# Turning the exponentials of an attention through scratch memory and VectorE instead of TensorE, with a second score tile in PSUM

## The chip, the core and the metric

One core of a Trainium2 chip runs the kernel alone, as one launch. The metric is the device time of that launch in microseconds (us). Engines are named as in the profile: PE (TensorE, with PEld for its weight loads), DVE (VectorE), ACT (ScalarE), POOL (GpSimd) and SP (SyncE, which here only waits for semaphores and issues DMAs). Each engine runs its own instruction list strictly in order; the lists meet only in semaphores.

## The reference, cut to what matters

The input is 16 images of 32x32 pixels and 128 channels, fp32. Each goes through two layers.

```
# layer 0: depthwise 3x3 convolution to 3C, 1x1 to 2C, gelu, 1x1 back to C, residual;
#          then 3x3 windowed local attention, residual
# layer 1: group norm (8 groups), then full attention over the 1024 pixels:
xf = xn.reshape(B, n, C)                                   # n = 1024
q, k, v = xf @ Wq + bq, xf @ Wk + bk, xf @ Wv + bv
attn = softmax(einsum('bnc,bmc->bnm', q, k) * C ** -0.5)   # 1024 x 1024 per image
out = einsum('bnm,bmc->bnc', attn, v) @ Wp + bp
return xn + out.reshape(B, H, W, C)
```

The change is in the full attention of layer 1: between the exponentials of a score tile, which come out with queries on the partitions, and the product with v, which needs keys on the partitions.

## The kernel before, in words

**Tiling.** The scores of one image are made in 8 tiles, `t` = 0 to 7, each 128 queries by 1024 keys (two PSUM banks). A tile goes through this chain: `scores(n, t)` on PE (6 matmuls); `row_max` on DVE (negated row maximum, out of PSUM); `exp` on ACT (PSUM to the SBUF tile `e`, with the row sums); `probs_t` on PE (8 transposes of 128x128 blocks of `e` into the PSUM tile `ps_t`); `et_hi_tile` on ACT (PSUM to `et_hi`, rounded to the fast matmul type fp32r); `et_lo_tile` on DVE (`ps_t` minus `et_hi`, the remainder). `values(n, j)` on PE multiplies the pair hi/lo of two tiles with the pair of v. Almost every product of the kernel is written as three fp32r matmuls over such hi/lo pairs (`mm3`, L438 to L443, which is why many groups of the profile stand at L441 to L443). On POOL one helper, `minus` (L1419, L1420), makes the remainders `t_lo`, `g_lo`, `h_lo` and `xn_lo`; both its operands lie in SBUF.

**Buffers.** Before the change there is one score tile in PSUM (`ps_s`), one tile `e`, one tile `ps_t`. `scores(t)` therefore waits for `exp(t-1)`, `exp(t)` for `probs_t(t-1)`, `probs_t(t)` for `et_lo_tile(t-1)`. `et_hi` and `et_lo` hold four tiles each, so tile `t` waits for `values` of tile pair `t/2 - 2`. Four more PSUM banks (`work`) are handed round by fixed plans (`BANK_PLAN`, `FILL_PLAN`, `DRAIN_PLAN`).

**Order.** The order of work of each engine is written out by hand as three lists of calls: `fill_program` (images 0 to 2 are started), `turn_program(it)`, run for it = 1 to 12, and `drain_program` (the last images). One turn works on four images at once: a = it (full attention, output), b = it + 1 (local attention, group norm, q, k, v of layer 1), c = it + 2 (convolution, gelu, q, k, v of layer 0), d = it + 3 (input and its Winograd transform). So in the steady state one turn finishes one image.

**Instructions of VectorE with both tensor operands in SBUF.** They matter below. In a turn there are ten larger ones: `transform_even` (2, L1602 and L1603), `transform_two` (2, L1612), `transform_ends` (2, L1621), `combine` (2, L1716), `combine_own` (2, L1723); and four tiny ones in the group norm (L1801, L1809, L1817, L1819). All others read PSUM with one operand, or have a single tensor operand.

**SP.** In a turn SP issues `store(a, 0)`, the four input loads of the next image (`load_x`), and `store(a, 1)`, each behind its wait.

```
            def probs_t(n, t):
                te.wait_ge(*e_ready.after(n, t))
                te.wait_ge(*et_lo_ready.after(n, t - 1))
                for kt in range(TILES):
                    mm = te.transpose(ps_t[:, kt * 128:(kt + 1) * 128], e[:, kt * 128:(kt + 1) * 128], ident)
```

Of the kernel before, what the change touches and what calls it, by code (L numbers as in the profile page):

```python
# [2227 lines left out]
```

## Time and profile before

| | us |
|---|---|
| three runs | 1071.11 median (1070.84 to 1073.47) |
| the profiled execution | 1070.88 |
| its span, first to last instruction | 1068.9 |
| PE busy | 1023.6 (96%) |
| DVE busy | 835.5 (78%) |
| ACT busy | 730.4 (68%) |
| POOL busy | 395.7 (37%) |
| mean granted clock of TensorE | 0.996 |

The page is read from the busy shares to the stages: the first score matmul of the drain stands at about 922 us, and a turn repeats every 63.7 us, so the twelve turns are by far the largest part. The chain that ended last is of little use here: much of it is "issue", time in which the engine waited for nothing that the profile shows.

### The profile page before, as it was taken

How to read it: one execution, taken by the hardware profiler on the slowest of the kernel's cores; microseconds unless marked ns; L12 is line 12 of the kernel's file. 1: busy time of each engine (PE TensorE's matmuls, PEld its weight loads, DVE VectorE, ACT ScalarE, POOL GpSimd, SP SyncE). 2: the span in 40 equal slices, each digit the busy share in tenths (PEclk: the TensorE clock that was granted, in tenths of full speed). 3: DMA queues.
4: the chain of work that ended last, by engine and by line, in shares of the span. 5: the costliest groups of instructions: out<-in, count | busy, mean ns of one | idle time of the engine just before them, and what ended most of it. 6: DMA issues, size and time to landing. Idle time of an engine off the chain costs nothing.

```text
span 1068.9 us, 21353 instructions
## 1 busy us (share of the span) xinstructions
PE 1023.6 (96%) x7092; PEld 937.6 (88%) x7092; DVE 835.5 (78%) x1628; ACT 730.4 (68%) x1382; POOL 395.7 (37%) x366
## 2 busy tenths in 40 slices
PE   4989999999999999999999999999999999999997
PEld 3877889899898999989899898989989899898986
DVE  6868888778787877887878788877877787777774
ACT  1576866757675776857767685776767667677754
POOL 4535250533507144260623516053260714423021
PEclk9899999999999999999999999999999999999999
DMA  5101010010201001020100101001010100000001
GB/s 91 21 2 21 2 30 11 10 31 1 40 0 29 10 10 29 0 39 0 24 16 10 29 0 29 10 10 29 0 39 0 29 10 10 10 1 11 11 11 30
DMA packets 85637, 18.64 MB, mean 17 GB/s; under 512 B 67552, under 2 KB 85472, under 8 KB 85600
## 3 DMA queue, kind: packets, MB, share of 16 engines
q1 hardware_dynamic: 84752, 17.77, 8.8%
q10 hardware_dynamic: 848, 0.39, 0.2%
q8 instruction: 22, 0.36, 0.1%
q14 instruction: 15, 0.12, 0.0%
HBM read 9.76 MB, written 8.39 MB: 17 GB/s over the span
## 4 chain that ended last, share of the span: by engine, by line
issue 43%; PE 29%; POOL 13%; DVE 9%; ACT 4%; DMA 0%; POOLq 0%; SPq 0%; DVEq 0%; ACTq 0%
PE work L441 6%; PE work L443 5%; PE work L442 5%; PE ps_t L604 4%; POOL t_lo L1420 3%; POOL d L1426 2%; ACT et_hi L1042 2%; POOL xn_lo L1420 2%; PE work L500 2%; DVE d L1602 2%; POOL g_lo L1420 2%; POOL r_tok L1474 1%; POOL r_tok L1477 1%; PE ps_s L441 1%; PE ps_s L443 1%
## 5 line engine op out<-in xcount | busy, mean ns | idle before, releaser
L1420 POOL TENSOR_TENSOR g_lo<-u,g_hi 128x512 fp32r<-128x512 f32 x60 | 76.8, 1283 | 415.1 <-ACT g_hi L951 415.0
L1854 DVE TENSOR_TENSOR et_lo<-ps_t,et_hi 128x1024 fp32r<-128x1024 f32 x128 | 156.1, 1220 | 52.1 <-ACT et_hi L1042 51.6
L1042 ACT ACTIVATE et_hi<-ps_t 128x1024 fp32r<-128x1024 f32 x128 | 130.9, 1022 | 91.0 <-PE ps_t L604 87.8
L441 PE MATMUL work<-t_lo,wc_hi 128*128 128x256 f32 x576 | 173.4, 301 | 4.4 <-DVE wc_lo L1668 4.4
L1848 DVE TENSOR_REDUCE nm<-ps_s 128x1 f32<-128x1024 f32 x124 | 150.9, 1217 | 22.8 <-PE ps_s L443 20.5
L443 PE MATMUL work<-t_hi,wc_hi 128*128 128x256 f32 x576 | 162.8, 283 | 0.0
L442 PE MATMUL work<-t_hi,wc_lo 128*128 128x256 f32 x576 | 162.6, 282 | 0.0
L441 PE MATMUL work<-et_lo,vv_hi 128*128 128x256 f32 x512 | 147.9, 289 | 0.2 <-ACT a_all L1049 0.2
L1032 ACT ACTIVATE e<-ps_s,nm 128x1024 f32<-128x1024 f32 x124 | 138.1, 1114 | 11.7 <-DVE nm L1848 9.2
L443 PE MATMUL work<-et_hi,vv_hi 128*128 128x256 f32 x512 | 144.4, 282 | 0.0
L442 PE MATMUL work<-et_hi,vv_lo 128*128 128x256 f32 x512 | 144.1, 281 | 0.0
L604 PE MATMUL ps_t<-const,e 128*128 128x128 f32 x1024 | 132.8, 273 | 3.4 <-DVE et_lo L1854 3.4
L604 PEld LDWEIGHTS ps_t<-const,e 128*128 128x128 f32 x1024 | 118.3, 141 | 17.3 <-ACT e L1032 3.6
L441 PEld LDWEIGHTS work<-t_lo,wc_hi 128*128 128x128 f32 x576 | 110.1, 191 | 5.5 <-issue 4.9
L442 PEld LDWEIGHTS work<-t_hi,wc_lo 128*128 128x128 f32 x576 | 110.1, 191 | 0.0
L443 PEld LDWEIGHTS work<-t_hi,wc_hi 128*128 128x128 f32 x576 | 109.6, 190 | 0.0
L441 PE MATMUL ps_s<-kk_lo,qq_hi 128*128 128x512 f32 x248 | 104.2, 420 | 0.4 <-ACT e L1032 0.3
L443 PE MATMUL ps_s<-kk_hi,qq_hi 128*128 128x512 f32 x248 | 98.2, 396 | 0.0
L442 PE MATMUL ps_s<-kk_hi,qq_lo 128*128 128x512 f32 x248 | 98.0, 395 | 0.0
L441 PEld LDWEIGHTS work<-et_lo,vv_hi 128*128 128x128 f32 x512 | 96.6, 189 | 1.3 <-issue 0.4
L442 PEld LDWEIGHTS work<-et_hi,vv_lo 128*128 128x128 f32 x512 | 96.5, 189 | 0.8
L443 PEld LDWEIGHTS work<-et_hi,vv_hi 128*128 128x128 f32 x512 | 96.4, 188 | 0.0
(184 smaller groups left out, 2415.7 us busy)
## 6 DMA issues: line engine op xcount, KB each, us to landing
x_in<-in_x SPq DMA_DIRECT2D x64, 128.0 KB, 3.4
out<-r_tok SPq DMA_DIRECT2D x32, 256.0 KB, 2.3
w_up_t<-in_L_conv_w_up SPq DMA_DIRECT2D x1, 384.0 KB, 3.8
const<-in_const ACTq DMA_DIRECT2D x1, 166.0 KB, 4.6
y<-in_L_conv_w_up ACTq DMA_DIRECT2D x1, 128.0 KB, 4.5
y<-in_L_conv_w_qkv SPq DMA_DIRECT2D x1, 128.0 KB, 4.7
const<-in_const ACTq DMA_DIRECT2D x1, 64.0 KB, 4.2
w_v<-in_L_conv_w_qkv SPq DMA_DIRECT2D x1, 64.0 KB, 2.8
```

The source lines that it names most:

```text
L441: te.matmul(dst, wh, xl, start=first, stop=False)
L442: te.matmul(dst, wl, xh, start=False, stop=False)
L443: return te.matmul(dst, wh, xh, start=False, stop=last)
L500: mm = te.matmul(bank("v", half, n)[:, t * 128:(t + 1) * 128], h[:, at:at + 128], w_v[:, :], start=True, stop=True)
L604: mm = te.transpose(ps_t[:, kt * 128:(kt + 1) * 128], e[:, kt * 128:(kt + 1) * 128], ident)
L1032: act.activation(e[:, :], score_tile(n, t)[:, :], ACT.Exp, bias=nm1[:, t:t + 1], accum_out=sum1[:, t:t + 1]) \
L1042: act.activation(et_hi[:, :, (t % 4) * 128:(t % 4 + 1) * 128], ps_t[:, :].rearrange("p (k c) -> p k c", k=TILES), ACT.Copy) \
L1420: return pool.tensor_tensor(dst, full, hi, ALU.subtract)
L1426: ins_ = pool.tensor_tensor(d2_of(n)[:, r], xp_of(n)[:, r + 2:r + 31:4, 1:1 + W], xp_of(n)[:, r:r + 29:4, 1:1 + W], ALU.subtract)
L1602: dve.scalar_tensor_tensor(d[:, 0], x[:, 1:30:4, 1:1 + W], -4.0, x[:, 3:32:4, 1:1 + W], ALU.mult, ALU.add)
L1848: dve.tensor_reduce(nm1[:, t:t + 1], score_tile(n, t)[:, :], AX.X, ALU.max, negate=True) \
L1854: dve.tensor_tensor(et_lo[:, :, cols_], ps_t[:, :].rearrange("p (k c) -> p k c", k=TILES), et_hi[:, :, cols_].bitcast(F32), ALU.subtract). ...
```

## The change

The eight PE transposes of a tile go. In their place the tile is written to a scratch tensor in DRAM and read back, so that one read brings 32 neighbouring keys' columns of all query blocks to one partition group, and a VectorE transpose (which works on blocks of 32x32) finishes the turn.

- `exp` writes `e` with its columns regrouped in runs of 32 (the same instruction, another output pattern). There are two tiles `e`, two tiles `e_by_keys`, two scratch areas `e_blocks`, used by t % 2.
- `move_out(n, t)` on SP waits for `exp(t)` and issues four stores of 32 partitions each (128 KB in runs of 1 KB). `move_in(n, t)` waits until all four have landed and issues one load of 512 KB (4 KB a partition).
- `et_turn(n, t)` on DVE waits for the load and transposes 128x1024 into the new SBUF tile `et_f`, in runs of 32.
- `et_hi_tile` on ACT now reads `et_f` in SBUF, not PSUM. `et_lo_tile` moves from DVE to POOL, reading `et_f` and `et_hi` in SBUF.
- The PSUM of `ps_t` becomes a second score tile: `scores(t)` waits for `exp(t-2)`. `exp(t)` waits for `et_turn(t-2)`.
- All lists and bank plans are written anew. `load_x(d)` stands in the turn where image d is transformed, no longer one turn ahead.

```diff
+        e = [sb(f"e_{k}", [128, PIX]) for k in range(2)]
+        e_by_keys = [sb(f"e_by_keys_{k}", [128, PIX]) for k in range(2)]
+        et_f = placed("et_f", [128, TILES, HALF], et_at + 4 * TILES * HALF)
...
-            return work_all[:, 0:PIX] if is_last(n) and t % 2 else ps_s
+            return (ps_s, ps_t)[t % 2]
...
+        e_blocks = nc.dram_tensor("e_blocks", (2, 128 * PIX), F32, kind="Internal").ap()
...
+            def move_out(n, t):
+                sp.wait_ge(*e_ready.after(n, t))
+                blocks = e_blocks[t % 2].rearrange("(a j q m) -> q j a m", a=4, j=32, q=4)
+                for part in range(4):
+                    sp.dma_start(blocks[part], e[t % 2][32 * part:32 * (part + 1), :].rearrange("j (a m) -> j a m", a=4)) \
+                      .then_inc(written[t % 2].handle, 16)
+
+            def move_in(n, t):
+                sp.wait_ge(*written[t % 2].after(n, t // 2))
+                sp.dma_start(e_by_keys[t % 2][:, :], e_blocks[t % 2].rearrange("(p c) -> p c", p=128)) \
+                  .then_inc(moved[t % 2].handle, 16)
...
-                if not is_last(n) or t == 0:
-                    te.wait_ge(*e_ready.after(n, t - 1))
...
+                te.wait_ge(*e_ready.after(n, t - 2))
...
-            def probs_t(n, t):
-                te.wait_ge(*e_ready.after(n, t))
-                te.wait_ge(*et_lo_ready.after(n, t - 1))
-                for kt in range(TILES):
-                    mm = te.transpose(ps_t[:, kt * 128:(kt + 1) * 128], e[:, kt * 128:(kt + 1) * 128], ident)
-                mm.then_inc(pe["t"].handle, 1)
...
             def exp(n, t):
                 act.wait_ge(*max1_ready.after(n, t))
-                act.wait_ge(*pe["t"].after(n, t - 1))
+                act.wait_ge(*et_ready.after(n, t - 2))
...
             def et_hi_tile(n, t):
+                cols_ = slice((t % 4) * 128, (t % 4 + 1) * 128)
+                act.wait_ge(*et_ready.after(n, t))
+                act.activation(et_hi[:, :, cols_], et_f[:, :, cols_], ACT.Copy).then_inc(et_hi_ready.handle, 1)
...
+            def et_lo_tile(n, t):
+                cols_ = slice((t % 4) * 128, (t % 4 + 1) * 128)
+                pool.wait_ge(*et_hi_ready.after(n, t))
+                minus(et_lo[:, :, cols_], et_f[:, :, cols_], et_hi[:, :, cols_].bitcast(F32)).then_inc(et_lo_ready.handle, 1)
...
+            def et_turn(n, t):
+
+                dve.wait_ge(*moved[t % 2].after(n, t // 2))
...
+                if t % 2 == 0:
+                    dve.wait_ge(*pe["pv"].after(n, t // 2 - 2))
                 cols_ = slice((t % 4) * 128, (t % 4 + 1) * 128)
...
+                dve.transpose(et_f[:, :, cols_].rearrange("p b (q j) -> p q b j", q=4),
+                              e_by_keys[t % 2][:, :].rearrange("p (q b j) -> p q b j", q=4, b=TILES)) \
+                   .then_inc(et_ready.handle, 1)
...
```

The new order of a turn, where the text below follows it (calls in their order, image letters as above, `out`/`in` for `move_out`/`move_in`):

```
SP:   out a0; in a0; out a1; in a1; out a2; out a3; in a2; in a3; load_x(d); out a4; out a5; in a4; in a5;
      out a6; out a7; in a6; in a7; store(a,0); store(a,1)
DVE:  row_max a1; local_mask_max b0; row_max a2; local_mask_max b1; local_rec b0; local_mask_max b2; halo_turn b0;
      local_rec b1; et_turn a0; row_max a3; sum_and_difference c(1); et_turn a1; halo_turn b1; sum_and_difference c(3);
      local_rec b2; row_max a4; local_mask_max b3; combine c(2); halo_turn b2; et_turn a2; row_max a5; et_turn a3;
      local_rec b3; combine c(1); combine_own c(0); combine_own c(3); end_row c(4); end_row c(5); halo_turn b3;
      y_half b0; row_max a6; et_turn a4; et_turn a5; row_max a7; y_half b1; h_half c0; channel_moments b;
      group_variance b; group_norm b; v_half c0; et_turn a6; output a0; et_turn a7; kk_lo b0; qq_lo b0; h_half c1;
      x_turn d0; kk_lo b1; x_turn d1; qq_lo b1; v_half c1; transform_even d; row_max b0; transform_two d; vv_lo b0;
      output a1; transform_ends d; vv_lo b1
ACT:  exp a1; ...; exp a2; local_scale b1; take c2; exp a3; local_scale b2; et_hi a0; et_hi a1; pt_pair b1;
      local_exp b3; exp a4; et_hi a2; pt_pair b2; exp a5; et_hi a3; local_scale b3; gelu c0; g_hi c0; gelu c1;
      a_part a0; g_hi c1; pt_pair b3; et_hi a4; exp a6; et_hi a5; exp a7; h_hi c0; gelu c2; ...; exp b0; ...
POOL: residual a0; et_lo a0; et_lo a1; et_lo a2; et_lo a3; g_lo c0; g_lo c1; et_lo a4; et_lo a5; inverse_deviation b;
      h_lo c0; g_lo c2; xn_lo b0; g_lo c3; xn_lo b1; et_lo a6; et_lo a7; h_lo c1; differences d; residual a1;
      transform d; t_lo d0; t_lo d1; t_lo d2
```

## Rows read from the trace of the kernel before

**Rows 1.** Stretches: us; PE, PEld, DVE, ACT, POOL busy; clock; DMA share; GB/s
```profile
404.30:468.20 63.90, 62.91 (x445) 58.05 (x444) 51.44 (x101) 45.06 (x86) 24.41 (x23) 1.00 0.08 16
851.30:1068.90 217.60, 206.71 (x1433) 187.72 (x1431) 158.78 (x310) 144.18 (x269) 61.79 (x55) 0.99 0.06 13
```

**Rows 2.** Timeline of SP's input loads (start, us, engine, line), five turns apart
```profile
276.62 2.55 SPq L381 DMA_DIRECT2D x_in<-in_x  x4
594.90 2.30 SPq L381 DMA_DIRECT2D x_in<-in_x  x4
```

**Rows 3.** Groups by line and form: busy us, mean ns, idle before and releaser
```profile
L1854 DVE TENSOR_TENSOR et_lo<-ps_t,et_hi 128x1024 fp32r<-128x1024 f32 x128 | 156.1, 1220 | 52.1 <-ACT et_hi L1042 51.6
L441 PE MATMUL ps_s<-kk_lo,qq_hi 128*128 128x512 f32 x248 | 104.2, 420 | 0.4 <-ACT e L1032 0.3
L1032 ACT ACTIVATE e<-ps_s,nm 128x1024 f32<-128x1024 f32 x124 | 138.1, 1114 | 11.7 <-DVE nm L1848 9.2 <-PE ps_t L604 2.2
L604 PE MATMUL ps_t<-const,e 128*128 128x128 f32 x1024 | 132.8, 273 | 3.4 <-DVE et_lo L1854 3.4
L1420 POOL TENSOR_TENSOR g_lo<-u,g_hi 128x512 fp32r<-128x512 f32 x60 | 76.8, 1283 | 415.1 <-ACT g_hi L951 415.0
L946 ACT ACT_TABLE_LOAD x18 | 23.1, 1283 | 0.3
L1596 DVE STREAM_TRANSPOSE xp<-x_in 128x512 f32<-128x512 f32 x30 | 21.0, 707 | 11.1 <-DMA x_in<-in_x 9.3
L1436 POOL TENSOR_TENSOR t_f<-d 128x256 f32<-128x256 f32 x15 | 11.4, 758 | 12.1 <-DVE d L1603 12.1
```

**Rows 4.** The output stores: KB each, median us to landing; issue durations in ns
```profile
out<-r_tok SPq DMA_DIRECT2D x32, 256.0 KB, 2.3
L397 SPq DMA_DIRECT2D out<-r_tok x32: 372/412/417, 139.6 to 1066.2; - x32
```

**Rows 5.** Half-microsecond stretches: under a weight load, under a store (columns as rows 1)
```profile
3.00:3.50 0.50, 0.00 (x0) 0.00 (x0) 0.00 (x0) 0.00 (x0) 0.09 (x2) 1.00 1.08 417
288.50:289.00 0.50, 0.50 (x4) 0.36 (x4) 0.16 (x1) 0.39 (x1) 0.50 (x1) 1.00 1.03 291
```

**Rows 6.** Timeline of POOL and DVE in one turn: start, us, engine, line
```profile
467.35 1.30 POOL L1420 TENSOR_TENSOR h_lo<-h,h_hi 128x512 fp32r<-128x512 f32 x1 [0.83 <-ACT h_hi L958]
467.43 1.49 DVE L1602 SCALAR_TENSOR_TENSOR d<-xp 128x256 f32<-128x256 f32 x1
468.85 0.41 DVE L1603 SCALAR_TENSOR_TENSOR d<-xp 128x256 f32<-128x256 f32 x1
...
473.23 2.53 DVE L1612 SCALAR_TENSOR_TENSOR t_f<-d 128x256 f32<-128x256 f32 x2
473.63 1.60 POOL L1420 TENSOR_TENSOR t_lo<-t_f,t_hi 128x512 fp32r<-128x512 f32 x1
...
477.94 1.18 DVE L1621 SCALAR_TENSOR_TENSOR t_f<-d 128x256 f32<-128x256 f32 x2
...
512.25 1.30 POOL L1474 TENSOR_TENSOR r_tok<-vv_hi,vv_lo 128x512 f32<-128x512 f32 x1
512.26 0.69 DVE L1790 TENSOR_TENSOR y<-work,h 128x512 f32<-128x512 f32 x1 [0.41 <-PE work L545]
513.62 1.28 POOL L1477 TENSOR_TENSOR r_tok<-r_tok,bp_row 128x512 f32<-128x512 f32 x1
513.96 0.96 DVE L1801 SCALAR_TENSOR_TENSOR moments<-moments 128x1 f32<-128x1 f32 x1
```

**Rows 7.** Durations of two lines, ns min/median/max, over all images
```profile
L1716 DVE SCALAR_TENSOR_TENSOR u<-u x30: 670/680/840, 39.3 to 941.8; 128x512 f32<-128x512 f32 x30
L1801 DVE SCALAR_TENSOR_TENSOR moments<-moments x16: 219/955/1019, 81.2 to 1014.3; 128x1 f32<-128x1 f32 x16
```

**Rows 8.** Timeline of ACT: first and last exponential after the twelve turns
```profile
929.46 1.10 ACT L1032 ACTIVATE e<-ps_s,nm 128x1024 f32<-128x1024 f32 x1
1054.98 1.11 ACT L1032 ACTIVATE e<-work,nm 128x1024 f32<-128x1024 f32 x1
```

More of the change, by code:

```diff
@@ L406, in fill_program @@
                 load_x(2)
+                move_out(0, 0)
+                move_in(0, 0)
+                move_out(0, 1)
+                move_in(0, 1)
+                move_out(0, 2)
+                move_in(0, 2)
+                move_out(0, 3)
+                move_in(0, 3)
+                move_out(0, 4)
+                move_in(0, 4)
+                move_out(0, 5)
+                move_out(0, 6)
+                move_in(0, 5)
+                move_in(0, 6)
                 load_x(3)
+                move_out(0, 7)
@@ L408, in fill_program @@
+                move_in(0, 7)
                 store(0, 0)
-                load_x(4)
                 store(0, 1)
             def turn_program(it):
-                a, d = it, it + 3
+                a, b, c, d = it, it + 1, it + 2, it + 3
+                move_out(a, 0)
+                move_in(a, 0)
+                move_out(a, 1)
+                move_in(a, 1)
+                move_out(a, 2)
+                move_out(a, 3)
+                move_in(a, 2)
+                move_in(a, 3)
+                load_x(d)
@@ L414, in turn_program @@
+                move_out(a, 4)
+                move_out(a, 5)
+                move_in(a, 4)
+                move_in(a, 5)
+                move_out(a, 6)
+                move_out(a, 7)
+                move_in(a, 6)
+                move_in(a, 7)
                 store(a, 0)
-                if has_next(d + 1):
-                    load_x(d + 1)
                 store(a, 1)
             def drain_program():
-                store(B - 3, 0)
-                store(B - 3, 1)
-                store(B - 2, 0)
@@ L423, in drain_program @@
-                store(B - 2, 1)
+                move_out(B - 3, 0)
+                move_in(B - 3, 0)
+                move_out(B - 3, 1)
+                move_in(B - 3, 1)
+                move_out(B - 3, 2)
+                move_in(B - 3, 2)
+                move_out(B - 3, 3)
+                move_in(B - 3, 3)
+                move_out(B - 3, 4)
+                move_in(B - 3, 4)
+                move_out(B - 3, 5)
+                move_in(B - 3, 5)
+                move_out(B - 3, 6)
+                move_in(B - 3, 6)
@@ new lines, in drain_program @@
+                move_out(B - 3, 7)
+                store(B - 3, 0)
+                move_in(B - 3, 7)
+                move_out(B - 2, 0)
+                move_in(B - 2, 0)
+                move_out(B - 2, 1)
+                move_in(B - 2, 1)
+                move_out(B - 2, 2)
+                move_in(B - 2, 2)
+                move_out(B - 2, 3)
+                move_in(B - 2, 3)
+                move_out(B - 2, 4)
+                store(B - 3, 1)
+                move_in(B - 2, 4)
+                move_out(B - 2, 5)
@@ new lines, in drain_program @@
+                move_in(B - 2, 5)
+                move_out(B - 2, 6)
+                move_in(B - 2, 6)
+                move_out(B - 2, 7)
+                move_in(B - 2, 7)
+                move_out(B - 1, 0)
+                store(B - 2, 0)
+                move_out(B - 1, 1)
+                move_in(B - 1, 0)
+                move_in(B - 1, 1)
+                move_out(B - 1, 2)
+                move_out(B - 1, 3)
+                move_in(B - 1, 2)
+                move_in(B - 1, 3)
+                store(B - 2, 1)
@@ L424, in drain_program @@
+                move_out(B - 1, 4)
+                move_out(B - 1, 5)
+                move_in(B - 1, 4)
+                move_in(B - 1, 5)
+                move_out(B - 1, 6)
+                move_out(B - 1, 7)
+                move_in(B - 1, 6)
+                move_in(B - 1, 7)
                 store(B - 1, 0)
                 store(B - 1, 1)
-            fill_program()
-            turn_program(1)
-            with sp.Fori(2, B - 4) as it:
-                turn_program(it)
-            turn_program(B - 4)
@@ L432, in _ @@
-            drain_program()
+            run(sp, fill_program, turn_program, drain_program)
             sp.wait_ge(*stored.after(B - 1, 1))
@@ new lines, in fill_program @@
+                local_exp(1, 1)
+                local_scale(1, 0)
+                take(2, 0, 1)
+                exp(0, 1)
+                t_hi_part(2, 1)
+                q_half(1, 1)
+                local_scale(1, 1)
+                pt_pair(1, 0)
+                exp(0, 2)
+                pt_pair(1, 1)
+                local_exp(1, 2)
+                et_hi_tile(0, 0)
+                t_hi_part(2, 2)
+                local_scale(1, 2)
+                take(2, 2, 3)
+                local_exp(1, 3)
@@ L1189, in fill_program @@
+                et_hi_tile(0, 1)
+                exp(0, 3)
+                et_hi_tile(0, 2)
+                vv_hi_half(0, 1)
+                exp(0, 4)
                 pt_pair(1, 2)
+                local_scale(1, 3)
                 gelu(2, 0)
+                pt_pair(1, 3)
+                g_hi_part(2, 0)
                 gelu(2, 1)
-                g_hi_part(2, 0)
-                et_hi_tile(0, 2)
+                gelu(2, 2)
                 g_hi_part(2, 1)
-                local_exp(1, 3)
@@ L1236, in turn_program @@
                 a, b, c, d = it, it + 1, it + 2, it + 3
+                exp(a, 1)
+                local_exp(b, 0)
+                local_scale(b, 0)
+                local_exp(b, 1)
+                local_exp(b, 2)
+                pt_pair(b, 0)
+                take(c, 0, 1)
+                exp(a, 2)
+                local_scale(b, 1)
+                take(c, 2, 3)
+                exp(a, 3)
+                local_scale(b, 2)
                 et_hi_tile(a, 0)
-                exp(a, 1)
-                take(c, 0, 1)
@@ new lines, in drain_program @@
+                exp(B - 3, 5)
+                g_hi_part(B - 1, 2)
+                exp(B - 3, 6)
+                h_hi_half(B - 1, 0)
+                et_hi_tile(B - 3, 4)
+                a_part(B - 3, 0)
+                xn_hi_half(B - 2, 0)
+                xn_hi_half(B - 2, 1)
+                a_part(B - 3, 1)
+                g_hi_part(B - 1, 3)
+                q_half(B - 1, 0)
+                k_half(B - 1, 0)
+                qq_hi_half(B - 2, 0)
+                kk_hi_half(B - 2, 0)
+                kk_hi_half(B - 2, 1)
@@ L2148, in drain_program @@
-                halo_turn(B - 1, 3)
-                et_lo_tile(B - 2, 5)
-                y_half(B - 1, 0)
+                local_rec(B - 1, 0)
+                et_turn(B - 2, 0)
+                local_rec(B - 1, 1)
+                halo_turn(B - 1, 0)
+                local_mask_max(B - 1, 2)
+                row_max(B - 2, 3)
+                halo_turn(B - 1, 1)
+                local_rec(B - 1, 2)
+                et_turn(B - 2, 1)
+                halo_turn(B - 1, 2)
+                local_mask_max(B - 1, 3)
@@ L2151, in drain_program @@
+                vv_lo_half(B - 2, 0)
+                row_max(B - 2, 4)
+                et_turn(B - 2, 2)
+                local_rec(B - 1, 3)
+                output(B - 3, 1)
+                row_max(B - 2, 5)
+                halo_turn(B - 1, 3)
+                y_half(B - 1, 0)
+                vv_lo_half(B - 2, 1)
+                et_turn(B - 2, 3)
                 y_half(B - 1, 1)
                 channel_moments(B - 1)
+                row_max(B - 2, 6)
                 group_variance(B - 1)
+                et_turn(B - 2, 4)
@@ L2181, in drain_program @@
+                et_turn(B - 1, 6)
+                et_turn(B - 1, 7)
                 output(B - 1, 0)
[L2182 removed]
                 output(B - 1, 1)
```

1032 lines of the change are left out of this document (478 added, 554 removed), and 59 rows, old and new, of tables (BANK_PLAN, DRAIN_PLAN, FILL_PLAN).

## The prediction

> **What bounds the kernel now.** I read the busy shares of the page first: PE 96%, DVE 78%, ACT 68%, POOL 37%. An average over stages proves nothing, so the next view is the busy time by stretch. Input loads five turns apart give the turn: (594.90 - 276.62) / 5 = 63.66 us [rows 2]. In one such turn PE is busy 62.9 of 63.9 us, DVE 51.4, ACT 45.1, POOL 24.4 [rows 1]. So in the steady state PE sets the pace and the others wait for it. Twelve turns are 764 of the 1070.9 us. The sum below is made against the profiled execution, 1070.88 us (span 1068.9), which lies 0.23 us under the median of the runs. The other 305 us are the fill and the last images; there too PE is busy, for 206.7 of the last 217.6 us [rows 1].
>
> **What goes.** The 1024 transposes keep PE busy for 132.8 us [rows 3], 1.04 us a tile, 8.3 us a turn. PE's floor of a turn falls from 62.9 to 54.6 us. If PE alone mattered the turns would give back 12 x 9 = 108 us.
>
> **What comes, by engine, per turn.**
>
> *DVE.* `et_lo` goes (1.22 us a tile), `et_turn` comes. The trace has a transpose of 128x512 at 0.707 us [rows 3], also with output in runs of 32. Bounds for 128x1024: 1.22 us if the second 512 columns cost what they cost an ordinary instruction (0.69 us for 512 [rows 6], 1.22 for 1024: +0.53 [rows 3]), twice 0.707 = 1.41 at the other end. I take 1.24, next to the row of the same width: a change of +0.2 us a turn, at most +1.5.
>
> *ACT.* `et_hi` reads SBUF in place of PSUM: nothing that matters in 45 us. But gelu and exp now alternate twice a turn (gelu, exp a6 and a7, gelu, exp b0) and a table load takes 1.28 us [rows 3]: two more, +2.6 us. ACT stands at 48 us, hidden, except that one load falls ahead of `exp a6`.
>
> *POOL.* Eight `et_lo` of 128x1024. The trace has 0.758 us for 256 and 1.283 for 512 elements [rows 3]: 1.283 + 2 x 0.525 = 2.33 us (2.57 if it were twice the 512). That is 18.7 us; POOL goes from 24.4 to 43 us a turn. It still has slack, yet this is the costly edit, for the next reason.
>
> *The lock between POOL and DVE.* A DVE instruction with both operands in SBUF stands still while POOL works. L1602 took 1.49 us from 467.43, until `h_lo` on POOL had ended at 468.65; its twin L1603 behind it took 0.41 [rows 6]. Two L1612 across POOL's instructions took 2.53 us, the pair L1621 with POOL idle 1.18 [rows 6]. L1801, 0.22 us when free, has a median of 0.955 [rows 7]. The addition out of PSUM at 512.26 took its usual 0.69 beside POOL [rows 6]. The Trainium skill's page SBUF — State Buffer, section Who interferes with whom, has this as a rule: a VectorE instruction with two SBUF inputs and a GpSimd instruction that reads SBUF lock each other out for the whole instruction. By that rule `et_lo` on DVE (one operand in PSUM) never took part, and `et_lo` on POOL does, for 2.33 us at a time; the trace agrees with the first half (the row at 512.26), and no run here shows the second yet.
>
> Priced from the rows: fourteen such instructions a turn. Today they lose (1.49 - 0.41) + (2.53 - 1.18) + (0.96 - 0.22) = 3.2 us. If they met POOL at random, each would lose the sum of half the squares of POOL's durations over the turn: (15 instructions of 512 elements, 6 of 256) (15 x 1.28² + 6 x 0.76²) / 2 = 14.0; 14.0 / 63.7 x 14 = 3.1 us, just about what they lose. After the change 8 x 2.33² / 2 = 21.7 is added: 35.7 / 62 x 14 = 8.1 us. But they don't meet at random: in the new order `et_hi` a2 and a3 follow closely on `et_turn` a2 and a3, and `combine` and two `combine_own` come right behind on DVE, so two of these wait for nearly a whole `et_lo` (4.3 us); `channel_moments` follows `et_lo` a5. Placed by hand so, the losses come to 13. I take 10, between the two, against 3.2 now.
>
> *The round trip through DRAM.* An issue takes SP 0.41 us [rows 4], some 0.48 with what lies between; four are 1.9. A store of 256 KB lands 2.3 us after its issue [rows 4], of which some 0.9 is data at 291 GB/s [rows 5]; so 1.4 fixed, and the last 128 KB of four lands 1.4 + 0.4 after its issue: 3.2 us for `move_out`. `move_in`: 512 KB at 417 GB/s, the best stretch of the trace [rows 5], is 1.26 us, at 291 it is 1.8: 2.7 to 3.2 after issue, I take 3.0. Together 6.3 us. Bounds: 5.7 if `move_out` takes 3.0 and the load runs at 417 GB/s; 8.7 if the last store takes the 2.3 us of one twice its size (3.7 in all) and the load, next to other traffic, half of 291 GB/s (5.0).
>
> Where does it show? `exp(t)` waits for `et_turn(t-2)`, so two tiles are under way, and SP holds `in a2` behind `out a3`, `in a4` behind `out a5`, `in a6` behind `out a7`. After `et_turn a1` ends, `exp a3` takes 1.3, `out a3` 1.9 of issue, `in a2` 3.0: `et_turn a2` can start 6.2 us later, and DVE has some 4.7 us of work till then (the calls between them in its new list, at the durations of the same calls in the turn of rows 6, as are the next two figures; `combine` with 0.68 [rows 7] is the typical one): a wait of 1.5. From `et_turn a3` to a4: 6.4 us against 6.4 of work: none. From a5 to a6: `et_hi`, a table load and two exponentials stretch it to 9.4, against 7: 2.5, which the locks of the group norm fill. At the turn's seam `out a0` queues on SP behind `store(a-1, 1)`, which waits for `output`; DVE has 8 us of work before it asks: none. What is queued behind a waiting `et_turn` is all of DVE: `row_max`, hence `exp`; the convolution's sums, hence gelu. I keep 3.5 us of waits and gaps a turn beside the locks. `load_x(d)`, moved into this turn, costs SP 2.5 us ahead of `out a4`, which isn't ready before, and its reader comes half a turn later: nothing, or half a us if its packets delay `out a4`.
>
> *Second score tile.* PE waits 0.4 us in all before its first score matmul [rows 3]: worth nothing today; it covers the longer chain of tomorrow.
>
> **Sum.** DVE of a turn: 51.4 - 3.2 (locks now) + 0.2 + 10 (locks after) + 3.5 = 61.9 us, above PE's 54.6: DVE with its waits becomes what ends last. Twelve turns: 12 x (61.9 - 63.7) = -21. After the last turn there is little to hide the round trip behind: the exponentials of 23 tiles lie 125.5 us apart there, first to last [rows 8]. A pair's loop is now 1.25 (exp) + 3.8 (two `move_out` issued) + 0.5 (load issued) + 3.0 + 1.24 = 9.8 us; 11.5 pairs make 113, 12 less. The tail behind the last `exp` gets the round trip and a slower `et_lo` for PE's transposes, +6. About -5. The fill, PE busy too, gives perhaps -5. Total 1070.9 - 31 = 1040 us.
>
> **Rivals.**
> *A, forecast:* the locks eat most of what PE gives back. Turn 60 to 64, 1015 to 1064 us.
> *B, the locks stay small,* as today's 3.2 us or little more, because DVE stands in waits anyway when POOL works. For it: the losses of the group norm are partly covered. Against: `combine` stands right behind `et_turn`. DVE 55 to 58, PE's floor 54.6: turn 57, 12 x -6.7 - 10 = -90: 980 us.
> *C, slower: the round trip is the bound.* Place: `et_turn` a2, a4, a6 on DVE, and the pairs of the last images. Each us beyond 6.3 adds about 3 us a turn, since three of the four pairs have no slack, 36 in all, and 12 us at the end: 1040 + 48x. It decides from 6.95 us; 7.5 gives 1098, 8 gives 1122. For it: five DMAs a tile where a turn had six in all, and stores, loads and input on one queue. Against: the traffic asked is 8 MB a turn, 135 GB/s, and 291 and 417 were seen.
> *D, the transpose takes 1.41,* not 1.24: +1.4 us a turn moves A by 16 us, still faster; that the PE work goes is sure from the diff.
>
> **Chances.** A 0.45, B 0.27, C 0.22 (locks of 13 with a round trip of 6.6 end there too), the rest around no change. What a measurement of this kernel can tell from no change is about 0.3%, 3.2 us. Faster 0.70 (B, most of A, D), same 0.08, slower 0.22. Likeliest 1040, its own range 1010 to 1064; with B down to its middle and C up to 7.5 us of round trip, 975 to 1100.
>
> **What would show it.** Right: PE busy near 890 us with waits in every turn; L1854 gone and a DVE transpose of 1.2 to 1.3 us x128; POOL `et_lo` at 2.3 us; `combine`, `combine_own` and L1801's successors with medians 1 us and more above 0.68 and 0.22 [rows 7]; turn 60 to 64 us. Wrong: `combine` at 0.68 (B); `et_turn` waiting for the DMA several us a turn (C); loads landing after 4 us or more (C); ACT or SP busy without a gap, which no step above allows for.

## The result, and the profile after

1129.45 us (median of 4 runs, 1122.80 to 1130.03) against 1071.14 for the kernel before on the same chip: the ratio is 1.0525, 95% interval 1.0483 to 1.0567. The change made the kernel slower by 58 us; 1040 was forecast, and the range ended at 1100.

First the busy shares of the page of the kernel after (1129.47 us, span 1127.7):

```profile
PE 965.2 (86%) x6068; PEld 852.9 (76%) x6068; DVE 905.2 (80%) x1628; ACT 749.6 (66%) x1402; POOL 714.5 (63%) x494
```

PE lost the transposes and is no longer what ends last; no engine is above 86%. So no engine's busy time explains the loss by itself, and the waits have to be looked at. To place them, the span is cut at `channel_moments` of image 2 and of image 12, ten turns apart (the `memset` of `stat_mark` on DVE marks them). First the kernel before, then after: us from and to, length, busy PE, PEld, DVE, ACT, POOL, granted clock, DMA share, GB/s.

```profile
195.48:832.05 636.57, 626.96 (x4402) 577.94 (x4402) 511.94 (x1002) 448.03 (x851) 241.84 (x221) 1.00 0.09 17
```

```profile
207.50:874.86 667.36, 585.82 (x3761) 519.44 (x3760) 561.14 (x1002) 468.87 (x871) 445.38 (x300) 0.98 0.53 142
```

Three stretches make up the 58.8 us between the two spans: up to image 2, +12.0 (207.50 - 195.48); the ten turns, +30.8 (66.74 us a turn instead of 63.66); the rest, +16.0 (252.8 instead of 236.9). In a turn DVE is now busy for 56.1 us (51.2 before) and idle for 10.6. The waits of DVE in those ten turns (engine, tile and line, who ended the wait: us in total, times, longest):

```profile
DVE et_f L1934 <- DMA e_by_keys<-e_blocks: 56.3, 39, 3.0
DVE r_tok L1947 <- POOL r_tok L1511: 17.9, 10, 1.9
DVE max_mark L1838 <- ACT pn L1023: 10.6, 10, 1.1
DVE gn L1891 <- POOL gn L1487: 6.6, 10, 0.7
DVE g_mom L1881 <- PE work L640: 6.0, 10, 0.8
...
```

`et_turn` (L1934) waits 5.6 us a turn for its load, and 4.1 us more are spread over four other places. The largest of these, `r_tok`, is new: `output` waits there for POOL's `residual`, which stands behind the last `et_lo` in POOL's list (17.9 us in ten turns; before the change DVE stood idle for 0.7 at this place). The groups that answer to [rows 3] and [rows 7] (busy us, mean ns, idle before):

```profile
L1449 POOL TENSOR_TENSOR et_lo<-et_f,et_hi 128x1024 fp32r<-128x1024 f32 x128 | 313.9, 2464 | 251.3 <-ACT et_hi L1073 251.3
L1934 DVE STREAM_TRANSPOSE et_f<-e_by_keys 128x1024 f32<-128x1024 f32 x128 | 157.5, 1237 | 103.6 <-DMA e_by_keys<-e_blocks 103.3
...
L1797 DVE SCALAR_TENSOR_TENSOR u<-u 128x512 f32<-128x512 f32 x30 | 56.4, 1919 | 0.0
...
L1790 DVE SCALAR_TENSOR_TENSOR u<-u 128x512 f32<-128x512 f32 x30 | 32.5, 1088 | 0.0
```

The transpose takes the 1.24 us that was forecast, `et_lo` 2.46 where 2.33 was. `combine_own` (L1797) needs 1.92 us, 0.68 when nothing holds it [rows 7]: the lock is there. The transfers (KB each, median us from issue to landing) took longer than forecast:

```profile
e_blocks<-e SPq DMA_DIRECT2D x512, 128.0 KB, 2.6
e_by_keys<-e_blocks SPq DMA_DIRECT2D x128, 512.0 KB, 4.1
```

One turn shows the trip tile by tile. SP's queue, then DVE (start, us):

```profile
417.87 15.00 SPq L399 DMA_DIRECT2D out<-r_tok  x2
433.26 1.80 SPq L410 DMA_DIRECT2D e_blocks<-e  x4
437.10 0.34 SPq L415 DMA_DIRECT2D e_by_keys<-e_blocks  x1
437.56 1.88 SPq L410 DMA_DIRECT2D e_blocks<-e  x4
442.44 0.34 SPq L415 DMA_DIRECT2D e_by_keys<-e_blocks  x1
443.70 6.45 SPq L410 DMA_DIRECT2D e_blocks<-e  x8
450.26 0.39 SPq L415 DMA_DIRECT2D e_by_keys<-e_blocks  x1
```

```profile
441.19 1.25 DVE L1934 STREAM_TRANSPOSE et_f<-e_by_keys 128x1024 f32<-128x1024 f32 x1 [1.18 <-DMA e_by_keys<-e_blocks]
...
445.82 1.25 DVE L1934 STREAM_TRANSPOSE et_f<-e_by_keys 128x1024 f32<-128x1024 f32 x1 [1.08 <-DMA e_by_keys<-e_blocks]
...
454.61 1.25 DVE L1934 STREAM_TRANSPOSE et_f<-e_by_keys 128x1024 f32<-128x1024 f32 x1 [2.81 <-DMA e_by_keys<-e_blocks]
```

Tile a1: stores issued from 437.56, load at 442.44, transpose at 445.82, 8.3 us behind the first store. Tile a2: the first four of the eight stores at 443.70, its load only at 450.26, because SP first waits for the exponential of a3 and issues that tile's stores; the transpose begins 10.9 us behind the first store and DVE has stood for 2.81 us.

### The profile page after: what moved, and what is told of

The parts are those of the page before. It is cut to its first block, busy times and chain, and to the rows that moved or that the text cites. A ratio compares the mean times of both kernels' runs of the same rounds, so it can differ in the third digit from the quotient of the medians.

```text
span 1127.7 us, 20253 instructions
## 1 busy us (share of the span) xinstructions
PE 965.2 (86%) x6068; PEld 852.9 (76%) x6068; DVE 905.2 (80%) x1628; ACT 749.6 (66%) x1402; POOL 714.5 (63%) x494
## 4 chain that ended last, share of the span: by engine, by line
POOL 36%; issue 33%; DMA 6%; DVE 3%; PE 3%; SPq 1%; ACT 1%; POOLq 1%; DVEq 0%; ACTq 0%
POOL et_lo L1449 16%; POOL g_lo L1449 4%; POOL d L1455 4%; DMA e_by_keys<-e_blocks 3%; POOL r_tok L1508 3%; DMA e_blocks<-e 2%; POOL h_lo L1449 2%; POOL xn_lo L1449 2%; POOL t_lo L1449 2%; POOL r_tok L1511 2%; SPq L410 1%; DVE et_f L1934 1%; PE work L528 1%; PE work L530 1%; PE work L529 1%
## 5 line engine op out<-in xcount | busy, mean ns | idle before, releaser
L1449 POOL TENSOR_TENSOR et_lo<-et_f,et_hi 128x1024 fp32r<-128x1024 f32 x128 | 313.9, 2464 | 251.3 <-ACT et_hi L1073 251.3
L1934 DVE STREAM_TRANSPOSE et_f<-e_by_keys 128x1024 f32<-128x1024 f32 x128 | 157.5, 1237 | 103.6 <-DMA e_by_keys<-e_blocks 103.3
L528 PE MATMUL work<-t_lo,wc_hi 128*128 128x256 f32 x576 | 168.8, 293 | 10.3 <-DVE nm L1841 7.4
L1073 ACT ACTIVATE et_hi<-et_f 128x1024 fp32r<-128x1024 f32 x128 | 133.6, 1055 | 29.4 <-DVE et_f L1934 29.4
L1066 ACT ACTIVATE e<-ps_s,nm 128x1024 f32<-128x1024 f32 x64 | 71.4, 1115 | 80.2 <-DVE et_f L1934 76.7
L1066 ACT ACTIVATE e<-ps_t,nm 128x1024 f32<-128x1024 f32 x64 | 71.2, 1113 | 50.8 <-DVE et_f L1934 40.2
L528 PE MATMUL ps_s<-kk_lo,qq_hi 128*128 128x512 f32 x128 | 57.6, 450 | 31.9 <-ACT e L1066 31.6
L1922 DVE TENSOR_REDUCE nm<-ps_s 128x1 f32<-128x1024 f32 x64 | 77.4, 1210 | 3.8 <-PE ps_s L530 3.6
L1449 POOL TENSOR_TENSOR t_lo<-t_f,t_hi 128x512 fp32r<-128x512 f32 x48 | 61.1, 1297 | 26.6 <-ACT t_hi L959 26.6
L1922 DVE TENSOR_REDUCE nm<-ps_t 128x1 f32<-128x1024 f32 x64 | 76.5, 1195 | 0.0
```

The source lines that it names most:

```text
L528: te.matmul(dst, wh, xl, start=first, stop=False)
L1066: act.activation(e[t % 2][:, :].rearrange("p (a b i) -> p b a i", a=4, b=TILES), score_tile(n, t)[:, :].rearrange("p (b a i) -> p b a i", ...
L1073: act.activation(et_hi[:, :, cols_], et_f[:, :, cols_], ACT.Copy).then_inc(et_hi_ready.handle, 1)
L1449: return pool.tensor_tensor(dst, full, hi, ALU.subtract)
L1922: dve.tensor_reduce(nm1[:, t:t + 1], score_tile(n, t)[:, :], AX.X, ALU.max, negate=True) \
L1934: dve.transpose(et_f[:, :, cols_].rearrange("p b (q j) -> p q b j", q=4), e_by_keys[t % 2][:, :].rearrange("p (q b j) -> p q b j", q=4, b= ...
```

## The experiments

The table gives each one's time with its ratio to the kernel before, and per turn, over the same ten turns, its length, the busy time of DVE and PE and what `et_turn` waited for `e_by_keys` (each a tenth of the stretch's row). The kernels of e1, e2, e3, e7 and e11 leave work out, as their texts say; the others do all of it.

| kernel | us | ratio, 95% | turn | DVE | PE | wait |
|---|---|---|---|---|---|---|
| before | 1071.14 | 1 | 63.7 | 51.2 | 62.7 | - |
| after | 1129.45 | 1.0525 (1.0483 to 1.0567) | 66.7 | 56.1 | 58.6 | 5.6 |
| e1_lo_cut | 1087.5 | 1.0134 (1.0105 to 1.0163) | 63.6 | 51.9 | 57.8 | 8.7 |
| e2_trip_cut | 1055.68 | 0.9854 (0.9834 to 0.9874) | 62.5 | 56.9 | 57.3 | 0 |
| e3_both_cut | 974.19 | 0.9094 (0.9075 to 0.9112) | 56.6 | 51.5 | 55.7 | 0 |
| e4_early_exp | 1101.8 | 1.0284 (1.0265 to 1.0302) | 64.9 | 57.0 | 58.4 | 2.8 |
| e5_fp32 | 1078.01 | 1.0073 (1.0049 to 1.0097) | 62.3 | 50.0 | 59.4 | 7.0 |
| e6_fp32_early | 1035.62 | 0.9681 (0.9641 to 0.9720) | 60.3 | 50.2 | 58.6 | 5.5 |
| e7_load_cut | 1071.18 | 0.9993 (0.9978 to 1.0007) | 63.2 | 56.4 | 57.8 | 1.4 |
| e8_unpaired | 1118.7 | 1.0434 (1.0413 to 1.0455) | 65.9 | 51.4 | 59.5 | 9.4 |
| e9_four | 1104.61 | 1.0299 (1.0278 to 1.0320) | 66.0 | 50.4 | 60.7 | 9.5 |
| e10_four_later | 1064.45 | 0.9934 (0.9913 to 0.9955) | 62.5 | 50.2 | 59.2 | 4.7 |
| e11_before_cut | 1019.92 | 0.9515 (0.9499 to 0.9530) | 59.9 | 50.5 | 57.7 | - |
| e12_four_pairs | 1023.25 | 0.9561 (0.9541 to 0.9581) | 59.6 | 50.0 | 58.4 | 2.2 |
| e13_loads_act | 1060.7 | 0.9872 (0.9828 to 0.9917) | 61.8 | 50.4 | 59.3 | 2.9 |
| e14_after_loads_act | 1150.44 | 1.0744 (1.0698 to 1.0790) | 67.0 | 52.2 | 58.9 | 6.3 |

**Lock or trip: a square of four** (e1_lo_cut, e2_trip_cut, e3_both_cut, and the kernel after). Theory T: the round trip binds. Rival L: the lock between GpSimd and VectorE does.

```
e1: - minus(et_lo[:, :, cols_], et_f[:, :, cols_], et_hi[:, :, cols_].bitcast(F32))
    + minus(et_lo[:, 0:1, cols_], et_f[:, 0:1, cols_], et_hi[:, 0:1, cols_].bitcast(F32))
    - (et_hi[:, kt, cols_], et_lo[:, kt, cols_]), kt == 0, ...        # in values
    + (et_hi[:, kt, cols_], et_hi[:, kt, cols_]), kt == 0, ...
e2: - for part in range(4):                                           # in move_out
    + for part in range(1):
    - sp.dma_start(e_by_keys[t % 2][:, :], e_blocks[t % 2].rearrange("(p c) -> p c", p=128))
    + sp.dma_start(e_by_keys[t % 2][:, 0:256], e_blocks[t % 2].rearrange("(p c) -> p c", p=128)[:, 0:256])
e3: both
```

> GpSimd forms et_lo over 128 of its 1024 columns only, in the same place and with the same waits and signals; the matmuls that would read it read et_hi a second time instead, so PE's work is the same in size. The round trip is untouched. In a turn of the changed kernel VectorE is busy 56 of 66.9 us, of which some 8 us are instructions stretched by the lock, and it waits for the rest, 5.7 us of it for e_by_keys. Theory T (the round trip is the bound): what the lock gives back becomes waiting for e_by_keys; 1105 to 1129 us, combine_own back at 0.7 us, the waits of et_turn for its DMA above 100 us in all. Rival L (the lock is the bound): 8 us of a turn go, 12 x 8 and some at both ends: 1010 to 1040 us.

> Of the round trip one store of the four is left (128 KB) and a load of 256 of the 1024 columns; the other columns of e_by_keys hold zeros from the start. All waits stay. The trip then is an issue of 0.4, a landing of 2.3, a load of 2.3: some 5.1 us instead of 8.2, and a quarter of the traffic. Theory T: 3.1 us less of trip gives back 3 us per us and turn until VectorE's own 56 us and what it waits for elsewhere bind: 1020 to 1050 us; the waits of et_turn for its DMA fall from 103 us to under 30. Rival L: 1105 to 1129 us.

> Both cuts together (et_lo over 128 columns, a quarter of the round trip). Both theories: VectorE falls to 48 us a turn and PE's 54.6 us come next: turns of 56 to 58 us, 970 to 1000 us. If neither the trip nor the lock is what binds, it stays above 1080.

Ten turns of e2_trip_cut and of e3_both_cut (columns as above), and e1_lo_cut's wait in its ten turns:

```profile
200.20:825.29 625.09, 572.80 (x3755) 515.23 (x3754) 569.42 (x1003) 470.68 (x872) 448.80 (x301) 0.98 0.23 51
```

```profile
192.96:758.49 565.53, 556.96 (x3760) 508.50 (x3759) 515.46 (x1003) 468.08 (x871) 290.14 (x300) 1.00 0.25 56
```

```profile
DVE et_f L1934 <- DMA e_by_keys<-e_blocks: 87.3, 64, 3.0
```

Without the lock DVE's busy time falls by 4.2 us a turn, but the wait for `e_by_keys` grows from 5.6 to 8.7, and the kernel is only 42 us faster: below T's range and above L's, so neither theory alone. Without the long trip 74 us go, just short of T's range. With both cuts 155 us go, more than 42 + 74, and only then is PE the bound (55.7 of 56.6 us), near the forecast's floor of 54.6. The two stand one behind the other in DVE's list: each covers a part of the other, and both must go before PE sets the pace. One thing is not separated: what e1 takes off is more than the lock. POOL's list gets shorter too, and the wait of `output` for `residual` falls from 17.9 to 0.6 us in ten turns. So read L as the price of `et_lo` on POOL, the lock (4.2 us a turn) and POOL's longer list (1.7) together.

**What the trip is made of** (e4, e7, e8). e7 cuts the load alone; e4 lets the exponential of tile t start when the stores of t-2 have landed, not when they have been read back; e8 puts each load right behind its own stores on SP.

```
e4: - act.wait_ge(*et_ready.after(n, t - 2))                    # in exp
    + act.wait_ge(*written[t % 2].after(n, t // 2 - 1))
    + sp.wait_ge(*et_ready.after(n, max(t - 2, -1)))            # in move_in; e_blocks has 4 tiles
e7: the load as in e2, the four stores whole
e8: - move_out(a, 2) / move_out(a, 3) / move_in(a, 2) / move_in(a, 3)   # and so on in the turn
    + move_out(a, 2) / move_in(a, 2) / move_out(a, 3) / move_in(a, 3)
```

> All the work is done; only what waits for what is looser: the exponential of tile t waits until the four stores of tile t-2 have landed, not until et_turn has read them back; the load of tile t waits for et_turn of tile t-2 instead, and scratch memory has four tiles. The order on every engine is as before. Theory T in the form that two tiles under way are too few for a trip of 8.2 us: ScalarE's 7 us of waiting for et_f in a turn go, and a turn loses 2 to 4 us: 1080 to 1110 us. Rival T2 (the trip binds through the order of VectorE's own list, where et_turn stands in front of the row maximum of a later tile): within 5 us of 1129. Rival L: within 5 us of 1129, too.

> The four stores whole, the load of 256 of 1024 columns only (the other columns of e_by_keys hold zeros): the load's landing falls from 4.1 to 2.4 us. At the 48 us that the forecast charged for each us of trip, 1129 - 1.7 x 48 = 1047, held up by the lock at the 1055 of e2_trip_cut: 1055 to 1075 us. If stores and load count by their share of the 4.1 us that e2_trip_cut took off (1.7 and 2.4): 1095 to 1105.

> All the work is done; in the turn SyncE issues the load of each tile right behind its stores, not behind the next tile's. In the trace of the changed kernel the load of a2 is held back 2.3 us by that; the loads of a4 and a6 are not. The stores of a3, a5, a7 now stand behind a wait for the landing of the tile before, and begin some 1 us later. Theory T: 1 to 2.5 us a turn: 1100 to 1118. If the order on SyncE is worth nothing: within 5 us of 1129.

The landings in e7_load_cut:

```profile
e_blocks<-e SPq DMA_DIRECT2D x512, 128.0 KB, 2.4
e_by_keys<-e_blocks SPq DMA_DIRECT2D x128, 128.0 KB, 2.4
```

From the first store's issue the trip is now 1.4 to the fourth issue (the 1.80 of four in SP's rows, less the last one's 0.4) + 2.4 + 2.4 = 6.2 us, against 1.4 + 2.6 + 4.1 = 8.1 in the kernel after. That is the trip that the forecast had taken, 6.3, and the kernel stands at 1071: a cut of 1.9 us gave 58 us, 31 for each us of trip where the forecast charged 48. e4 fell where T had it (1101.8), though a turn lost only 1.9 us. e8 gave back 11, just outside its range, and not by the trip alone: `et_turn` waited more in it (9.4 us a turn), while DVE's busy time fell to 51.4, because `et_lo` now fell beside other instructions (`combine_own` 0.76 us in place of 1.92). Between these two kernels the price of the lock hangs on a few us of phase.

**The forecast's other ground: what PE's relief is worth** (e11, the kernel before with one transpose of eight).

```
- for kt in range(TILES):                                        # in probs_t
+ for kt in range(TILES if is_first(n) and t == 0 else 1):
```

> The kernel before with one of the eight PE transposes of each tile (all eight in the first tile alone); what the others would have turned is left out, everything else stays. It shows what taking the transposes off PE is worth by itself, and how near VectorE comes to its own busy time of 51.4 us a turn once PE has only some 55.5. The forecast let VectorE's turn be its busy time and the new waits alone: by that, a turn of 55 to 56 us (PE), about 965 us. If VectorE keeps 5 us of waits that a busy PE covered before, as the remainder of e2_trip_cut says: 57 to 59 us a turn, 985 to 1010.

```profile
191.85:790.94 599.09, 576.87 (x3843) 514.30 (x3842) 505.15 (x1001) 448.16 (x851) 242.20 (x221) 1.00 0.09 18
```

That is 51 us less than before, short of the second of the expectations too. PE has 2 us of slack a turn here, and DVE, busy for 50.5 of 59.9 us, does not close up: it keeps waiting for other engines (its named waits sum to 8.5 us a turn: `et_hi` 1.7, `vv_hi` 1.4, and eight shorter ones). So in the order and with the buffers of the kernel before, relieving PE alone does not give the 108 us of PE's floor. This holds for that order only: e3_both_cut, with the new lists and the second score tile, takes 974, 97 us below the kernel before. Whether the lists or the score tile make this difference was not tried.

**Taking `et_lo` away for good** (e5, e6). A plain fp32 product needs no split of its operand, so `et_hi`, `et_lo` and `vv_lo` go, and the work is all done. (The slices of the two `residual` calls are left out here.)

```
- te.wait_ge(*et_lo_ready.after(n, 2 * j + 1))                   # in values
+ te.wait_ge(*et_ready.after(n, 2 * j + 1))
- mm = mm3(bank("pv", j, n)[:, 0:256], (vv_hi[:, kt, :], vv_lo[:, kt, :]),
-          (et_hi[:, kt, cols_], et_lo[:, kt, cols_]), kt == 0, kt == TILES - 1)
+ mm = te.matmul(bank("pv", j, n)[:, 0:256], vv_f[:, kt, :], et_f[:, kt, cols_],
+                start=kt == 0, stop=kt == TILES - 1)
- pool.tensor_tensor(r_tok, vv_hi, vv_lo, ALU.add)               # in residual
- pool.tensor_tensor(r_tok, r_tok, bp_row, ALU.add)
+ pool.tensor_tensor(r_tok, vv_f, bp_row, ALU.add)
e6: this and e4 together
```

> All the work is done, without the split of the turned exponentials: values multiplies et_f by an unsplit v in plain fp32, so et_hi (8 x 1.06 us a turn on ScalarE), et_lo (8 x 2.46 us on GpSimd) and vv_lo go, and the round trip stays. PE: 32 fp32 products of 256 columns in place of 96 of fp32r; a fp32 product of 204 columns shows two rows 172 ns apart in the trace of e3_both_cut, so 256 should take some 430 ns against 3 x 119: 13.8 us a turn in place of 11.4, PE's floor goes from 54.6 to 57. Theory T+L (lock and trip lie one behind the other on VectorE): the lock goes as in e1_lo_cut, and the chain behind et_turn is two instructions shorter: 1070 to 1090 us. If the trip alone held the turn in e1_lo_cut, nothing below 1080.

> e5_fp32 and e4_early_exp together. Effects that only add up: 1129 - 42 - 28 = about 1060 us. Theory T+L says that each cut is worth more beside the other, as e3_both_cut showed (155 us against 42 + 74): 1030 to 1050 us.

Both came out as T+L had it, e5 only just: its interval (1076.6 to 1081.8 us) holds the 1080 above which the trip alone would have left it. e5's products on PE (two rows for each product):

```profile
331.81 3.62 PE L685 MATMUL work<-et_f,vv_f 128*128 128x256 f32 x16
```

226 ns a row, 64 rows a turn: 14.5 us against 96 x 119 ns = 11.4 in fp32r, so PE pays 3 us a turn and ACT, POOL and DVE lose 7, 22 and 6. e6, at 1035.62, is faster than both kernels, and e5 and e4 together gave 94 us where 51 + 28 would only add up to 79.

**The order on SP** (e9, e10, e12, e13, e14). e9 is e6 with four buffers and e8's order; e10 moves `et_turn` of a0 to a3 and a5 behind one more `row_max` on DVE, likewise in the last images, and lets the last image's loads follow their own stores too; e12 is e10 with SP's old pairs, in the last image as well; e13 and e14 issue the loads on ACT.

```
e9:  e, e_by_keys, written, moved: [t % 4]; e_blocks: [t] of 8; SP's turn as in e8
e10: - et_turn(a, 0) / row_max(a, 3) / ... / et_turn(a, 1) / ... / row_max(a, 4)
     + row_max(a, 3) / ... / et_turn(a, 0) / ... / row_max(a, 4) / et_turn(a, 1)
e12: e10, SP's turn: out a2, out a3, in a2, in a3 (as in the changed kernel)
e13: e12, e14: the changed kernel; move_in out of SP's lists, into ACT's some 3 us of work behind its exp
```

> e6_fp32_early with four buffers for e and for e_by_keys (in the memory that et_hi leaves), eight tiles of scratch memory, and SyncE's loads right behind the stores as in e8_unpaired; the lists of the engines stay. e6_fp32_early turns in 60.3 us with PE busy for 58.6 and VectorE waiting 5.6 for e_by_keys. If it was the two buffers that held it: 59 us a turn, 1010 to 1025 us. If it is VectorE's own list, which puts et_turn in front of a later row maximum: within 8 us of 1035.

> e9_four with VectorE's list changed in the turn and in the last images: each et_turn stands behind one row maximum more, so three to four tiles are under way, and the last image's loads too follow their stores directly. If the order of VectorE's list is what makes the trip show: a turn of 58 to 59 us, near PE's 57 to 58, and 10 us less in the last images: 990 to 1015 us. If PE already sets the pace: like e9_four.

> e10_four_later with SyncE's lists as in the changed kernel again (two tiles' stores, then their two loads). In e9_four and e10_four_later the stores of a4 and a5 began 3.7 and 6 us after their exponentials, because SyncE stood in the wait for a landing. If that order cost e9_four its 69 us: a turn of 58 to 59.5 us and 1000 to 1030 us. If the earlier exponentials or the four buffers are to blame: above 1050.

> e12_four_pairs with the loads issued by ScalarE, each some 3 us of ScalarE's work behind its exponential; SyncE has the stores, the input and the output alone. ScalarE is busy 40 us of a turn and each issue takes it 0.4 us, 3.3 a turn. If SyncE's queue in order is a part of the trip: exponential to first store falls to 0.1 us for nearly every tile, 990 to 1015 us. If ScalarE, waiting for landings, holds back its exponentials as SyncE held back the stores: 10 to 40 us more than e12_four_pairs.

> The changed kernel itself, its loads issued by ScalarE at about the same distance behind their exponentials; all else as it is. If SyncE's order is a large part of the trip's price (e8_unpaired gave back 10 us): 1090 to 1110 us. If it is the transfers: within 10 us of 1129, since stores and loads take what they take whoever issues them.

e9 missed by 80 us, to the wrong side, and e10, which had to gain from DVE's list, by 50. One turn of SP's waits in e9, then in e12:

```profile
SPq L398 <- DVE r_tok L1848: 20.4, 2, 12.6
SPq L415 <- DMA e_blocks<-e: 19.4, 8, 2.9
SPq L409 <- ACT e L1066: 1.8, 1, 1.8
```

```profile
SPq L398 <- DVE r_tok L1848: 17.4, 2, 12.6
SPq L415 <- DMA e_blocks<-e: 9.4, 5, 2.8
SPq L409 <- ACT e L1066: 6.7, 3, 3.8
```

With a load behind its own stores SP stands 19.4 us a turn waiting for landings, and hardly ever for an exponential: SP had become a serial engine of its own, some 5 us a tile, and the stores of a4 and a5 began 3.7 and 6 us late (the four input loads, 3.35 us of issues in e9, stand in the same queue ahead of them). In pairs one wait covers two tiles. That e12, which differs from e10 in SP's lists alone, is 41 us faster shows it. Ten turns of e12, the fastest here that does all the work (0.9561 of before):

```profile
199.60:795.65 596.05, 584.22 (x3438) 516.04 (x3439) 500.01 (x982) 394.98 (x790) 221.87 (x200) 1.00 0.60 159
```

PE is busy for 58.4 of 59.6 us: it sets the pace again. Loads on ACT only moved the standing queue. e13 lost 37 us on e12, as its second expectation had it; e14 missed both, 21 us slower than the kernel after. In its ten turns ACT's own work stood behind the landings:

```profile
ACT e L1021 <- DMA e_blocks<-e: 33.8, 10, 3.4
ACT pt L987 <- DMA e_blocks<-e: 27.6, 10, 3.0
...
ACT p L969 <- DMA e_blocks<-e: 15.7, 10, 1.7
```

These three make 7.7 us a turn (8.5 with a fourth, `u`, left out above), and the next exponential is among them. A queue that no compute engine shares was not tried.

## Why the prediction was wrong

Rival C, to which it gave 0.22, is nearest to what happened: the round trip took 8.1 us, and C's formula gives 1040 + 48 x (8.1 - 6.3) = 1126 for it. That this comes so near 1129 is partly luck. With the trip of the forecast the kernel takes 1071 (e7), not 1040, and each us beyond costs 31, not 48; and the trip is not the only bound, as the square shows. The prediction's own upper bound of the trip, 8.7 us, covered the 8.1; its range went no further than 7.5. Point by point:

- **PE's floor, 54.6 us:** right where the waits are gone (55.7 busy in e3). In the kernel after PE is busy for 58.6 us a turn, and 965.2 in all where "near 890" was named as a sign of being right. The granted clock fell: 0.964 in the mean (0.996 before), 0.98 in the ten turns, 0.93 behind them (1.00 before in both). In the turn shown above PE was busy for 6.5 of the 10 us from 455 us, and over the next 10 us the clock is 0.66, a mean of its levels 2.4 and 1.2 GHz. By these means the clock accounts for at most 36 of the 75 us (an estimate: 0.036 x 1127.7 less 0.004 x 1068.9); the rest was not traced. **The transpose, 1.24; `et_lo`, 2.33; POOL, 43 us a turn:** right (1.24, 2.46, 44.5).
- **The locks, 10 us a turn:** the mechanism right, the size too high. DVE free of locks was put at 48.4 (51.4 - 3.2 + 0.2); it is busy for 56.1, so they take 7.7 by that figure, and e3's 51.5 leaves 3.1, the share of the kernel before, once `et_lo` is cut. The Trainium skill's page SBUF — State Buffer, section Who interferes with whom, has it that two SBUF inputs make a VectorE instruction stand while GpSimd reads SBUF; the half that no row had shown is shown now (`combine_own` 1.92 us beside an `et_lo` of 2.46).
- **The round trip, "Together 6.3 us":** this step failed first. The four issues took what was forecast; a store lands 2.6 us after its issue in the median, where 1.8 was said of the last of four, and the load 4.1, not 3.0. The fixed part of a store had been got by taking 0.9 us of data off the 2.3 us of a store twice its size; a lone 128 KB store lands in 2.1 (e2, e3), one of four in 2.4 among short loads (e7), and in 2.6 among whole ones. The load had been priced by the rates of two half microseconds of the trace [rows 5]; 3.0 us after issue is the least of 128, and 4.1 the median, because the next tile's stores or the twin's load run beside it (median 3.5 where only stores do, 4.3 where another load does). The Trainium skill's page DMA: Bandwidth & Descriptors, section Anatomy of one DMA — SWDGE (gpsimd) path, gives some 2.0 us and bytes / 436 GB/s for a transfer issued by GpSimd: for the load an estimate of 3.2 us, near its least here and not near its median; no run here issues one from GpSimd. e7 puts a number on the step: with the trip of the forecast the kernel takes 1071, so 58 of the 89 us by which the forecast was off are the trip's size, the locks being as they are.
- **Waits of 3.5 us a turn:** 10.6. At `et_turn` they came to 5.6. a2's was placed rightly (2.81 where 1.5 was said), and a4 and a6 show none, as said. Two were called none: at the seam `out a0` stands behind `store(a-1, 1)` (433.26 in the rows above, the exponential having ended at 430.94), and DVE waits 1.18 for it and 1.08 for a1. The others, 4 to 5 us, were left out altogether, as if DVE's busy time were DVE's floor. 1.8 of them come from POOL's longer list, of which the prediction said that it still has slack. The kernel before showed 12 us of idle DVE a turn, read as what PE's load makes; e11 shows that 9 of them stay in that kernel's order when PE is relieved.
- **SP "holds in a2 behind out a3":** right as a place (450.26), and worth 11 us when taken away (e8, the smaller lock included); that the opposite order would make SP itself the bound was not seen before e9.
- **Fill -5, last images -5:** some +5 and +16. The first of the 23 exponentials behind the twelve turns starts 42.5 us later than before (971.92 us against 929.46 [rows 8]); twelve turns at 3.1 us make 37 of that, which leaves some 5 for the fill. The 23 lie 130.0 us apart, where 113 was forecast and 125.5 stood before; behind the last one 25.8 us follow where 13.9 did, so the tail grew by 12, not by 6. The pair's loop of the last image was put at 9.8 us. Its exponentials of even tiles:

```profile
1077.10 1.11 ACT L1066 ACTIVATE e<-ps_s,nm 128x1024 f32<-128x1024 f32 x1 [5.06 <-DVE et_f L1934]
...
1087.77 1.11 ACT L1066 ACTIVATE e<-ps_s,nm 128x1024 f32<-128x1024 f32 x1 [4.38 <-DVE et_f L1934]
...
1099.27 1.12 ACT L1066 ACTIVATE e<-ps_s,nm 128x1024 f32<-128x1024 f32 x1 [5.06 <-DVE et_f L1934]
```

  10.7 and 11.5 us apart. With the short trip of e2 the rest behind the ten turns takes 226.4 us in place of 252.8. The tail hangs on `et_lo` as well: 23.0 us in e2, 17.7 in e3. In the four stretches of 10 us from 1080 us the granted clock is 0.67 to 0.84; no run separates what that costs here.

The sum of a turn then reads 48.4 + 7.7 + 10.6 = 66.7 where 48.4 + 10 + 3.5 = 61.9 stood: the locks 2.3 less, the waits 7.1 more. What stays open: how the 4 us of the other waits would shrink by another order of DVE's list, how much of the 12 us up to image 2 is the trip (7.3 us less in e2) and how much the order of the new lists, and what the second score tile is worth by itself.

## What to carry to other kernels

A round trip through DRAM inside a loop is priced by landings beside its own traffic, every transfer of its kind in flight, not by the best stretch seen; what is left of it can be hidden in part by letting the next tile start earlier (e4, 28 us). When the engine that bounds a loop is relieved, the next bound is the next engine's busy time plus the waits that it will keep. Cutting the relieved work out of the kernel before, in one run, shows these waits ahead of building the replacement, for the order of that kernel (59.9 us a turn in e11; the new order came to 56.6 in e3). Two causes that stand one behind the other on one in-order engine each look small alone (42 and 74 us) and must be cut together (155).

## What the runs showed of the hardware

- A 512 KB load from scratch memory lands 3.0 to 3.3 us after its issue with little or nothing beside it (the least of the kernel after, and the median of e14's loads that run alone), 3.8 beside the next tile's four stores (e9), and 4.2 to 4.8 in the median of the tiles whose loads are issued in pairs (e12).
- A queue that waits for landings is an engine with a busy time: a wait of 2.4 us and five issues made SP some 5 us a tile (e9), and on ACT such waits cost 8.5 us a turn (e14).
- With the same `et_lo` and the same instructions DVE was busy for 56.1 us a turn in one order of SP's list and 51.4 in another (e8): the lock's price is a matter of phase.
- A plain fp32 product of 256 columns takes 2 x 226 ns, 1.27 times its three fp32r products of 119 ns, and spares the split on three other engines.
